# A batched GNN and GRU on one core: four batches in flight, and states turned by block transposes through device memory

## The chip, the core and the metric

The kernel runs on one core of a Trainium2 chip. The metric is device time in microseconds (us), from the start of the program to its end; lower is better. A core has five engines that run their own instruction streams and meet only at semaphores: TensorE (PE, matrix products, with its weight loads shown as PEld), VectorE (DVE), ScalarE (ACT), GpSimd (POOL) and SyncE (SP), which here only issues transfers (DMA).

## The reference

Sixteen batches of 512 nodes with 128 features. A first layer mixes each node with the mean of its neighbours, then a layer norm. Then five GRU layers in a row, each fed with the sum over a node's incoming edges; then a residual, the node mask and a second layer norm. All is float32.

```python
adj_norm = adj / (sum(adj, -1, keepdims) + 1e-8)
h = relu(concat([x, adj_norm @ x]) @ weight + bias)
x = layernorm(x + h)
A = (adj != 0)
h = x
for l in range(5):
    m = h @ weight[l]
    agg = einsum('bij,bid->bjd', A, m)
    gi = agg @ w_ih.T + b_ih;  gh = h @ w_hh.T + b_hh
    r = sigmoid(i_r + h_r);  z = sigmoid(i_z + h_z);  n = tanh(i_n + r * h_n)
    h = (1 - z) * n + z * h
out = layernorm(x + h * mask)
```

## The kernel before

Products are made from pairs of float32r parts: `x_hi` (a rounded copy, written by ACT) and `x_lo` (the rest, a subtraction on DVE or POOL). A product is then three matmuls, hi by hi, lo by hi and hi by lo. The weights of message and input gates are multiplied together at the start (`wc`), so a layer sums the states over the edges first.

The work is cut into **units**: one GRU layer of one batch. A unit on TensorE is 26 matmuls 512 columns wide: 8 for the edge sum into `ps_tok` (lines 1292 and 1299, stationary `tok_hi` and `tok_lo`, moving `edges`), 9 state products (`state_products`: `ps_hn`, `ps_r`, `ps_z` from `h_hi`, `h_lo`), and 9 gate products from `agg_hi`, `agg_lo` (`ps_r`, `ps_z`, `ps_in`). The other engines then do, for a unit:

- ACT: `agg_hi`, `r_gate`, `z_gate`, the tanh in `ps_in`, `h_hi` (not after layer 4), `tok_hi`;
- DVE: `agg_lo`, `r_hn`, `ps_in` plus `r_hn` (line 1020), (z - 1) n (line 1059), the new state `h` (line 962), `tok_lo`;
- POOL: `z_h` = z h (line 604) and `h_lo` (line 594, not after layer 4).

A state `h` lies with features on the partitions, while the next edge sum wants it with tokens (nodes) on the partitions. So TensorE turns it (line 1330: four 128x128 transposes against `ident` into `ps_tok`), ACT copies `tok_hi` out of the bank and DVE makes `tok_lo` from the bank. Only the last state of a batch goes another way: a DVE block transpose of 32x32 blocks (line 1131), one transfer to `passage` in device memory, and four transfers back to `last_rows` (lines 472 and 475), which together turn it whole.

A **window** has five slots, and each slot holds at most one unit. `UNITS` gives for each slot (how many batches back, which layer). A window also prepares the next batch: parts of its adjacency (`adjt_hi`, `adjt_lo`), its products, neighbour sums, row sums, layer norm (`x1`), the turned `x1` (`first_state` in slot 4) and its parts (`tok_lo` from `x1` on POOL at line 585, `h_lo[0]` at line 599). It also finishes an old batch (`pre2`, `stats2`, `cent2`, `y_out`). `FIRST_WINDOWS` and `LAST_WINDOWS` list the slots where batches are few. Windows 3 to 14 are one loop body. Every engine's order is the order of the code: each `window` function walks through the slots and tests conditions, and each engine waits at semaphores in that order. Two units of one batch have two units of others between them.

```python
UNITS = ((0, 0), (1, 2), (2, 4), (0, 1), (1, 3))
```

## Time and profile before

| | us |
|---|---|
| median of 3 runs (lowest, highest) | 625.54 (624.91, 625.80) |
| the profiled execution: its own time | 624.76 |
| its span (first to last instruction) | 623.0 |
| PE, DVE, ACT, POOL busy in the span | 604.4, 515.1, 411.3, 366.5 |

A row of a timeline gives start, duration, engine, line, operation and, in brackets, the idle time just before it with what ended it. A row of a group gives count, busy time and mean duration of one. TensorE's granted clock is full all through the middle of the span. Matmuls overlap their neighbours, so the step from one matmul to the next is the difference of their starts, not the duration shown.

### The profile page before, as it was taken

The page shows a single profiled execution, that of the slowest core. Times are in us where ns is not written, and L with a number is a line of the kernel's source. Part 1 is how long each engine was busy: PE and PEld are TensorE (multiplying, and loading weights), DVE is VectorE, ACT ScalarE, POOL GpSimd, SP SyncE. Part 2 cuts the span into 40 slices and gives each one's busy share as a digit, 9 for nine tenths or more (in the row PEclk, how much of TensorE's full clock was granted, in tenths as well). Part 3 has the DMA queues.
Part 4 walks back from the last instruction along what each step waited for, and adds up shares of the span by engine and source line. Part 5 has one row for each costly group of instructions (what it writes and reads, how often), then busy time and mean ns, then how long its engine had stood idle before and what let it go on. Part 6 is the DMA issues. An engine that isn't in the chain of part 4 may idle for free.

```text
span 623.0 us, 10141 instructions
## 1 busy us (share of the span) xinstructions
PE 604.4 (97%) x2877; PEld 492.6 (79%) x2877; DVE 515.1 (83%) x1177; ACT 411.3 (66%) x777; POOL 366.5 (59%) x299
## 2 busy tenths in 40 slices
PE   6999999999999999999999999999999999999993
PEld 5677888888888888888888888888888888887772
DVE  5987978897988879798897979889798887967677
ACT  4866776858667585766758576685866758564551
POOL 0644555757666575765658576576766657555343
PEclk9999999999999999999999999999999999999997
DMA  8531222231232323223231331333124131010101
GB/s 270 213 102 68 101 69 102 99 104 52 84 134 68 101 68 121 80 84 114 88 101 51 99 120 67 118 100 102 51 84 135 67 101 34 17 34 1 51 1 52
DMA packets 48080, 54.63 MB, mean 88 GB/s; under 512 B 2880, under 2 KB 27968, under 8 KB 48064
## 3 DMA queue, kind: packets, MB, share of 16 engines
q1 hardware_dynamic: 47792, 54.31, 26.3%
q8 instruction: 7, 0.11, 0.1%
q10 hardware_dynamic: 272, 0.13, 0.1%
q14 instruction: 9, 0.07, 0.0%
HBM read 46.57 MB, written 7.86 MB: 87 GB/s over the span
## 4 chain that ended last, share of the span: by engine, by line
PE 91%; DVE 4%; DMA 1%; ACT 1%; issue 1%; SPq 1%; POOL 0%; POOLq 0%; DVEq 0%
PE ps_tok L1292 12%; PE ps_tok L1299 12%; PE ps_r L1157 6%; PE ps_r L1158 6%; PE ps_r L1159 6%; PE ps_z L1159 6%; PE ps_z L1158 6%; PE ps_z L1157 6%; PE ps_tok L1152 5%; PE ps_b L1157 3%; PE ps_b L1158 3%; PE ps_b L1159 3%; PE ps_in L1157 3%; PE ps_hn L1159 3%; PE ps_in L1158 3%; PE ps_in L1159 3%
## 5 line engine op out<-in xcount | busy, mean ns | idle before, releaser
L594 POOL TENSOR_TENSOR h_lo<-h,h_hi 128x512 fp32r<-128x512 f32 x64 | 82.9, 1295 | 107.5 <-ACT h_hi L624 107.5
L604 POOL TENSOR_TENSOR z_h<-z_gate,h 128x512 f32<-128x512 f32 x80 | 110.0, 1374 | 43.1 <-ACT z_gate L801 43.1
L624 ACT ACTIVATE tok_hi<-ps_tok 128x512 fp32r<-128x512 f32 x63 | 37.7, 598 | 96.2 <-PE ps_tok L1152 96.2
L1292 PE MATMUL ps_tok<-edges,tok_hi 128*128 (+1 forms) x320 | 87.9, 397 | 0.7 <-ACT tok_hi L624 0.7
L1136 DVE SCALAR_TENSOR_TENSOR r_hn<-ps_hn,gru_bias,r_gate 128x512 f32<-128x512 f32 x80 | 59.9, 748 | 34.5 <-ACT r_gate L791 33.4
L1299 PE MATMUL ps_tok<-edges,tok_lo 128*128 (+1 forms) x320 | 87.7, 396 | 0.0
L724 ACT ACTIVATE ps_in<-ps_in,gru_bias 128x512 f32<-128x512 f32 x80 | 52.8, 660 | 52.8 <-DVE ps_in L1020 52.7
L544 POOL TENSOR_TENSOR adjt_lo<-adjt_in,adjt_hi 128x512 fp32r<-128x512 f32 x56 | 71.8, 1302 | 4.2 <-ACT adjt_hi L624 4.2
L1292 PEld LDWEIGHTS ps_tok<-edges,tok_hi 128*128 128x128 f32 x320 | 59.8, 188 | 15.4 <-ACT tok_hi L624 0.9
L1299 PEld LDWEIGHTS ps_tok<-edges,tok_lo 128*128 128x128 f32 x320 | 59.9, 188 | 14.8 <-DVE tok_lo L827 0.3
L827 DVE TENSOR_TENSOR tok_lo<-ps_tok,tok_hi 128x512 fp32r<-128x512 f32 x63 | 43.6, 692 | 27.9 <-ACT tok_hi L624 27.9
L1059 DVE SCALAR_TENSOR_TENSOR ps_in<-z_gate,ps_in 128x512 f32<-128x512 f32 x80 | 55.2, 690 | 11.9 <-ACT ps_in L724 10.6
L791 ACT ACTIVATE r_gate<-ps_r,rz_bias 128x512 f32<-128x512 f32 x80 | 54.9, 686 | 14.2 <-PE ps_r L1159 11.4
L1020 DVE TENSOR_TENSOR ps_in<-ps_in,r_hn 128x512 f32<-128x512 f32 x80 | 56.0, 700 | 8.0
L827 DVE TENSOR_TENSOR agg_lo<-ps_tok,agg_hi 128x512 fp32r<-128x512 f32 x80 | 55.0, 688 | 4.3 <-ACT agg_hi L624 4.3
L624 ACT ACTIVATE agg_hi<-ps_tok 128x512 fp32r<-128x512 f32 x80 | 47.9, 598 | 15.2 <-PE ps_tok L1299 14.1
L962 DVE TENSOR_TENSOR h<-z_h,ps_in 128x512 f32<-128x512 f32 x80 | 54.4, 680 | 1.2
L801 ACT ACTIVATE z_gate<-ps_z,rz_bias 128x512 f32<-128x512 f32 x80 | 55.0, 687 | 0.5
L624 ACT ACTIVATE h_hi<-h 128x512 fp32r<-128x512 f32 x77 | 48.1, 625 | 7.2 <-DVE h L962 7.1
L550 POOL TENSOR_TENSOR rstd<-var,minus_half 128x4 f32<-128x4 f32 x15 | 15.3, 1021 | 48.2 <-DVE var L925 48.2
L1152 PEld LDWEIGHTS ps_tok<-ident,h 128*128 128x128 f32 x252 | 30.7, 140 | 10.7 <-issue 2.3
L1152 PE MATMUL ps_tok<-ident,h 128*128 128x128 f32 x252 | 38.0, 273 | 0.7 <-DVE agg_lo L827 0.3
(146 smaller groups left out, 1574.2 us busy)
## 6 DMA issues: line engine op xcount, KB each, us to landing
adjt_in<-in_adj_t_dram SPq DMA_DIRECT2D x14, 1024.0 KB, 5.3
adj_in<-in_adj_dram SPq DMA_DIRECT2D x14, 1024.0 KB, 5.4
x_in<-in_x_dram SPq DMA_DIRECT2D x16, 256.0 KB, 2.8
xt_in<-in_x_t_dram SPq DMA_DIRECT2D x15, 256.0 KB, 2.6
out_dram<-y_out SPq DMA_DIRECT2D x15, 256.0 KB, 2.3
passage<-last_blocks SPq DMA_DIRECT2D x14, 256.0 KB, 2.0
last_rows<-passage SPq DMA_DIRECT2D x56, 64.0 KB, 2.0
adjt_in<-in_adj_t_dram SPq DMA_DIRECT2D x4, 256.0 KB, 4.6
```

Of the source, the lines that this page charges most:

```text
L544: nc.gpsimd.tensor_tensor(adjt_lo[:, j, :], adjt_in[:, j, :], raw(adjt_hi[:, j, :]), ALU.subtract).then_inc(s_adjt_lo, 1)
L594: nc.gpsimd.tensor_tensor(h_lo[new][:], h[new][:], raw(h_hi[new][:]), ALU.subtract).then_inc(s_h_lo, 1)
L604: nc.gpsimd.tensor_tensor(z_h[:], z_gate[:], h[own][:], ALU.mult).then_inc(s_zh, 1)
L624: return nc.scalar.activation(dst, src, ACT.Copy)
L827: return nc.vector.tensor_tensor(dst, src, raw(hi), ALU.subtract)
L1136: nc.vector.scalar_tensor_tensor(out=r_hn[:], in0=ps_hn[:], scalar=bhh_cols[:, 2:3], in1=r_gate[:], op0=ALU.add, op1=ALU.mult).then_inc(s_ ...
L1152: return nc.tensor.transpose(dst, src, ident[:])
L1157: nc.tensor.matmul(dst, lhs_hi, rhs_hi, start=start, stop=False)
L1158: nc.tensor.matmul(dst, lhs_hi, rhs_lo, start=False, stop=False)
L1159: return nc.tensor.matmul(dst, lhs_lo, rhs_hi, start=False, stop=stop)
L1292: nc.tensor.matmul(ps_tok[:], tok_hi[:, c * P:(c + 1) * P], edges_from(c, unit[0]), start=c == 0, stop=False)
L1299: last = nc.tensor.matmul(ps_tok[:], tok_lo[:, c * P:(c + 1) * P], edges_from(c, unit[0]), start=False, stop=c == C - 1)
```

## The change

Four batches are in flight: `UNITS` becomes layer 0 of the newest batch, layer 4 of the one three back, layer 3 of two back, layer 2 of one back and layer 1 of the newest, so that three units of others stand between two of a batch. The lists of first and last windows follow, windows 4 to 14 are the loop, and there is one window more. In windows 3 to 15 every unit in slots 1 to 4 (51 units) takes its tokens from a moved state: DVE transposes the blocks of each new state into one buffer `blocks`, SP sends them to `passage[k]` and fetches them to `rows[k]` (k is the layer they are for; 5 is the end), ACT makes `tok_hi` from `rows[k]` one slot ahead, and POOL makes `tok_lo`. TensorE's transposes of those units go, and so does DVE's `tok_lo`. The other 13 units of layers 1 to 4 are turned as before. The last state of batch 13 is now turned by TensorE, where it was moved before.

```diff
-UNITS = ((0, 0), (1, 2), (2, 4), (0, 1), (1, 3))
+UNITS = ((0, 0), (3, 4), (2, 3), (1, 2), (0, 1))
...
 FIRST_WINDOWS = (((0, 0), None, None, None, (0, 1)),
-                 ((0, 0), (1, 2), (0, 1), None, (1, 3)))
-LAST_WINDOWS = (((0, 0), (1, 2), (0, 1), (2, 4), (0, 2)),
-                ((2, 3), (1, 3), (2, 4), None, None),
-                (None, (2, 4), None, None, None))
+                 ((0, 0), (1, 2), (0, 1), None, (1, 3)),
+                 ((0, 0), (1, 2), (2, 4), (0, 1), None),
+                 ((0, 0), None, (2, 3), (1, 2), (0, 1)))
+LAST_WINDOWS = (((3, 4), (1, 2), None, None, None),
+                ((3, 3), (2, 3), (3, 4), None, None),
+                (None, (3, 4), None, None, None))
+FIRST_MOVED = ((2, 2), (2, 3), (2, 4), (3, 1), (3, 3), (3, 4))
...
+def is_moved(batches, n, slot):
+    return 3 <= n < batches and slot > 0
...
+            def pass_on(w, slot):
+                k = w.unit_before(slot)[1] + 1
+                sp.wait_ge(s_blocks, w.moved(slot))
+                sp.dma_start(passage[k][:], blocks[:].rearrange("p q c j -> p (q c j)")).then_inc(s_passed, 16)
+                sp.wait_ge(s_passed, w.value(lambda n: 16 * moved_states(B, n, slot)))
                 for q in range(Q):
...
+                    sp.dma_start(rows[k][q * SQ:(q + 1) * SQ, :, :, :].rearrange("i f c j -> i f (c j)"),
+                                 passage[k].rearrange("(f i) (q m) -> i f q m", f=Q, q=Q)[:, :, q, :]
+                                 ).then_inc(s_rows[k], 16)
...
+                if w.moves(0):
+                    pass_on(w, 0)
                 if w.loads():
...
                     load_xt(b)
+                if w.moves(1):
+                    pass_on(w, 1)
+                if w.loads():
                     sp.wait_ge(s_adjt_lo, w.prepared(C, C) if w.first > 0 else C)
                     load_adjt(b)
+                if w.moves(2):
+                    pass_on(w, 2)
...
+                if w.moves(3):
+                    pass_on(w, 3)
                 if w.loads():
...
                     load_x(b)
...
                     load_adj(b)
+                if w.moves(4):
+                    pass_on(w, 4)
...
+                    if w.next_moved(slot):
+
+                        pool.wait_ge(s_tok_hi, w.turned(slot + 2))
+                        nc.gpsimd.tensor_tensor(tokens(tok_lo), rows_by_tokens(w.unit(slot + 1)[1]),
+                                                tokens(raw(tok_hi[:])), ALU.subtract).then_inc(s_tok_lo, 1)
...
+            def row_sum_of(c, of, earlier):
+
+                if earlier is not None:
+                    act.wait_ge(s_row_sum, earlier)
...
+                    if w.next_moved(slot):
+
+                        k = w.unit(slot + 1)[1]
+                        act.wait_ge(s_rows[k], w.rows(4 * 16, k))
+                        evacuate(tokens(tok_hi), rows_by_tokens(k)).then_inc(s_tok_hi, 1)
...
+                    if w.moves(slot):
+
+                        dve.wait_ge(s_h, w.units(slot))
+                        if w.first > 2 or slot > 0:
+                            dve.wait_ge(s_passed, w.value(lambda n: 16 * (moved_states(B, n, slot) - 1)))
+                        nc.vector.transpose(blocks[:].rearrange("p q c j -> p c q j"),
+                                            h[w.home_made(slot)][:].rearrange("p (c q j) -> p c q j", c=C, q=Q)
+                                            ).then_inc(s_blocks, 1)
...
-                    if unit:
+                    if unit and w.next_turned(slot):
                         pe.wait_ge(s_agg_lo, w.units(slot + 1))
...
                         wi_hi, wi_lo = wc_hi[:, layer, :], wc_lo[:, layer, :]
+                        pe.wait_ge(s_agg_lo, w.units(slot + 1))
```

Beside these, the four scratch copies of the row sums become one (so each row sum waits for the one before it), `stats1` in slot 3 comes whole behind `agg_lo`, `pre2` moves from slot 1 to slot 0, and the finishing of a batch comes one window later.

On TensorE, in slot 2 of the loop, from the last state product to the gate products, before:

```order
L1159 MATMUL ps_z<-h_hi4,whh_lo 128x512
...
L1152 MATMUL ps_tok<-ident,h1 128x128 [waits s_h,s_agg_lo]
L1152 MATMUL ps_tok<-ident,h1 128x128 x3
L1157 MATMUL ps_r<-agg_hi,wc_hi 128x512
L1158 MATMUL ps_r<-agg_lo,wc_hi 128x512
```

and now:

```order
L1240 MATMUL ps_z<-h_hi3,whh_lo 128x512
...
L1238 MATMUL ps_r<-agg_hi,wc_hi 128x512 [waits s_agg_lo]
L1239 MATMUL ps_r<-agg_lo,wc_hi 128x512
```

The four transposes are gone, and the gate products wait for `agg_lo` themselves. The same holds in slots 0, 1 and 3.

On TensorE, at the end of window 2, from the gates of slot 3 on (`h3` is a state that slot 4 turns into tokens), before:

```order
L1152 MATMUL ps_tok<-ident,h3 128x128 [waits s_h,s_agg_lo]
L1152 MATMUL ps_tok<-ident,h3 128x128 x3
L1157 MATMUL ps_r<-agg_hi,wc_hi 128x512
...
L1157 MATMUL ps_in<-agg_hi,wc_hi 128x512 [waits s_h]
...
L1292 MATMUL ps_tok<-edges,tok_hi 128x512 [waits s_tok_lo]
L1292 MATMUL ps_tok<-edges,tok_hi 128x512 x3
L1299 MATMUL ps_tok<-edges,tok_lo 128x512 x4
L1157 MATMUL ps_hn<-h_hi3,whh_hi 128x512 [waits s_rhn,s_h_lo]
```

and now, over the end of window 2 into slot 0 of window 3 (`x1` is the new batch's first state):

```order
L1238 MATMUL ps_in<-agg_hi,wc_hi 128x512 [waits s_h]
...
L1233 MATMUL ps_b1<-ident,x1 128x128 [waits s_x1]
L1233 MATMUL ps_b1<-ident,x1 128x128 x3
L1370 MATMUL ps_tok<-edges,tok_hi 128x512 [waits s_x1_hi,s_edges]
L1370 MATMUL ps_tok<-edges,tok_hi 128x512 x3
L1377 MATMUL ps_tok<-edges,tok_lo 128x512 [waits s_x1_lo]
L1377 MATMUL ps_tok<-edges,tok_lo 128x512 x3
L1238 MATMUL ps_hn<-h_hi0,whh_hi 128x512 [waits s_rhn,s_h0_lo]
```

The whole unit of slot 4 is gone from between the gates of slot 3 and the new batch's first unit. Slot 1 of window 3 likewise has only its neighbour sums left.

On GpSimd, in slots 2 and 3 of the loop, before:

```order
L559 TENSOR_TENSOR rstd2<-var2,minus_half 128x4 [waits s_var2]
L563 TENSOR_TENSOR cent2<-pre2,mv2 128x512
...
L567 TENSOR_TENSOR y_out<-cent2,rstd2 128x512 [waits s_cent2]
...
L594 TENSOR_TENSOR h_lo3<-h3,h_hi3 128x512 [waits s_h_hi]
...
L604 TENSOR_TENSOR z_h<-z_gate,h4 128x512 [waits s_z]
...
L550 TENSOR_TENSOR rstd1<-var1,minus_half 128x4 [waits s_var1]
...
L604 TENSOR_TENSOR z_h<-z_gate,h1 128x512 [waits s_z]
```

and now:

```order
L649 TENSOR_TENSOR tok_lo<-rows2,tok_hi 128x512 [waits s_tok_hi]
...
L618 TENSOR_TENSOR rstd2<-var2,minus_half 128x4 [waits s_var2]
L622 TENSOR_TENSOR cent2<-pre2,mv2 128x512
...
L626 TENSOR_TENSOR y_out<-cent2,rstd2 128x512 [waits s_cent2]
...
L668 TENSOR_TENSOR z_h<-z_gate,h3 128x512 [waits s_z]
L649 TENSOR_TENSOR tok_lo<-rows1,tok_hi 128x512 [waits s_tok_hi]
...
L609 TENSOR_TENSOR rstd1<-var1,minus_half 128x4 [waits s_var1]
...
L658 TENSOR_TENSOR h_lo4<-h4,h_hi4 128x512 [waits s_h_hi]
...
L668 TENSOR_TENSOR z_h<-z_gate,h2 128x512 [waits s_z]
```

A `tok_lo` stands at the head of both slots, and the `h_lo` of slot 2 is now in slot 3, behind `rstd1` and ahead of `z_h` (on ACT its `h_hi` now stands in slot 3 ahead of `r_gate`).

## Rows read from the trace of the kernel before

**Rows 1.** The page, its head and its section 1.

```profile
span 623.0 us, 10141 instructions
...
PE 604.4 (97%) x2877; PEld 492.6 (79%) x2877; DVE 515.1 (83%) x1177; ACT 411.3 (66%) x777; POOL 366.5 (59%) x299
```

**Rows 2.** Busy time of each engine in two stretches: window 2, and one loop window.

```profile
core 0: us, PE busy (x) PEld busy (x) DVE busy (x) ACT busy (x) POOL busy (x), PEclk, DMA share, GB/s
71.00:108.30 37.30, 37.30 (x180) 30.61 (x180) 30.65 (x61) 27.31 (x53) 20.69 (x17) 1.00 0.23 79
300.90:337.87 36.97, 36.97 (x180) 30.44 (x179) 31.57 (x73) 25.55 (x49) 23.84 (x19) 1.00 0.29 92
```

**Rows 3.** Timeline of PE: the turn in slot 2; slots 3 and 4 begin.

```profile
314.50 0.60 PE L1152 MATMUL ps_tok<-ident,h 128*128 128x128 f32 x4
314.85 0.48 PE L1157 MATMUL ps_r<-agg_hi,wc_hi 128*128 128x512 f32 x1
315.16 0.40 PE L1158 MATMUL ps_r<-agg_lo,wc_hi 128*128 128x512 f32 x1
315.40 0.40 PE L1159 MATMUL ps_r<-agg_hi,wc_lo 128*128 128x512 f32 x1
...
317.02 1.10 PE L1292 MATMUL ps_tok<-edges,tok_hi 128*128 x4
...
323.49 1.10 PE L1292 MATMUL ps_tok<-edges,tok_hi 128*128 x4
```

**Rows 4.** Groups of one shape: the turn, `tok_lo`, the block transpose, a GpSimd subtraction.

```profile
L1152 PE MATMUL ps_tok<-ident,h 128*128 128x128 f32 x252 | 38.0, 273 | 0.7 <-DVE agg_lo L827 0.3
L827 DVE TENSOR_TENSOR tok_lo<-ps_tok,tok_hi 128x512 fp32r<-128x512 f32 x63 | 43.6, 692 | 27.9 <-ACT tok_hi L624 27.9
L1131 DVE STREAM_TRANSPOSE last_blocks<-h 128x512 f32<-128x512 f32 x14 | 9.9, 706 | 0.0
L594 POOL TENSOR_TENSOR h_lo<-h,h_hi 128x512 fp32r<-128x512 f32 x64 | 82.9, 1295 | 107.5 <-ACT h_hi L624 107.5
```

**Rows 5.** The page, section 6: transfers, KB each, us to landing.

```profile
adj_in<-in_adj_dram SPq DMA_DIRECT2D x14, 1024.0 KB, 5.4
...
passage<-last_blocks SPq DMA_DIRECT2D x14, 256.0 KB, 2.0
last_rows<-passage SPq DMA_DIRECT2D x56, 64.0 KB, 2.0
```

**Rows 6.** Timeline of SP: issues of one moved state.

```profile
328.36 0.35 SPq L472 DMA_DIRECT2D passage<-last_blocks  x1
330.41 1.76 SPq L475 DMA_DIRECT2D last_rows<-passage  x4
```

**Rows 7.** Timeline: slot 4 and the start of slot 0.

```profile
324.48 1.43 DVE L931 TENSOR_SCALAR x<-pre,mv,rstd 128x128 f32<-128x128 f32 x4
...
326.43 0.69 DVE L827 TENSOR_TENSOR agg_lo<-ps_tok,agg_hi 128x512 fp32r<-128x512 f32 x1
...
326.75 1.29 POOL L585 TENSOR_TENSOR tok_lo<-x,tok_hi 128x512 fp32r<-128x512 f32 x1 [1.70 <-ACT tok_hi L624]
...
327.03 0.68 DVE L962 TENSOR_TENSOR h<-z_h,ps_in 128x512 f32<-128x512 f32 x1
...
327.74 0.63 ACT L624 ACTIVATE h_hi<-h 128x512 fp32r<-128x512 f32 x1 [0.55 <-DVE h L962]
327.78 0.48 PE L1157 MATMUL ps_r<-agg_hi,wc_hi 128*128 128x512 f32 x1
...
330.04 1.30 POOL L599 TENSOR_TENSOR h_lo<-h,h_hi 128x512 fp32r<-128x512 f32 x1 [0.29 <-ACT h_hi L624]
...
331.82 0.39 PE L1157 MATMUL ps_hn<-h_hi,whh_hi 128*128 128x512 f32 x1
```

**Rows 8.** Timeline of POOL: `adjt_lo` of a window's second half, slot 1.

```profile
302.43 2.56 POOL L544 TENSOR_TENSOR adjt_lo<-adjt_in,adjt_hi 128x512 fp32r<-128x512 f32 x2
```

**Rows 9.** Line 948 (`edges`): shortest, median and longest in ns; one pair in slot 1.

```profile
L948 DVE TENSOR_SCALAR edges<-adj_in x56: 412/421/1443, 55.0 to 536.8; 128x512 f32 x48, 128x512 fp32r<-128x512 f32 x8
...
308.25 1.67 DVE L948 TENSOR_SCALAR edges<-adj_in 128x512 f32 x2
```

More of the change, by code:

```diff
@@ L306, in program @@
         Q = P // SQ
-        last_blocks = sb("last_blocks", [P, Q, C, SQ])
-        passage = nc.dram_tensor("passage", [P, N], F32, kind="Internal").ap()
-        last_rows = sb("last_rows", [P, Q, C, SQ])
+        KINDS = range(1, LAYERS + 1)
+        blocks = sb("blocks", [P, Q, C, SQ])
+        passage = {k: nc.dram_tensor(f"passage{k}", [P, N], F32, kind="Internal").ap() for k in KINDS}
+        rows = {k: sb(f"rows{k}", [P, Q, C, SQ]) for k in KINDS}
         ps_tok = bank("ps_tok")
@@ L406, in all_windows @@
         def all_windows(window, eng):
-            for n in range(3):
+            for n in range(4):
                 window(Window(B, n))
-            with eng.Fori(0, B - 4) as trip:
-                window(Window(B, 3, trip))
-            for n in range(B - 1, B + 3):
+            with eng.Fori(0, B - 5) as trip:
+                window(Window(B, 4, trip))
+            for n in range(B - 1, B + 4):
                 window(Window(B, n))
@@ L1052, in window @@
                         low_part(agg_lo[:], ps_tok[:], agg_hi[:]).then_inc(s_agg_lo, 1)
+                    if slot == 1 and w.ends_by_rows() and not w.prepares():
+                        stats2_of_batch()
                     if slot == 2 and w.idles():
@@ L1062, in window @@
                         new_state(slot)
-                    if w.unit(slot) and not before_candidate(w, slot):
-                        dve.wait_ge(s_agg_hi, w.units(slot + 1))
+                    if w.summed(slot) and not before_candidate(w, slot):
+                        v, s = w.summed(slot)
+                        dve.wait_ge(s_agg_hi, v.units(s + 1))
                         low_part(agg_lo[:], ps_tok[:], agg_hi[:]).then_inc(s_agg_lo, 1)
```

174 lines of the change are left out of this document (90 added, 84 removed).

## The prediction

> **What bounds the kernel now.** I read the page's head first: TensorE is busy for 604.4 of 623.0 us [rows 1], the next engine, DVE, for 515.1. Then the busy time by stretch: in a loop window TensorE is busy for all of its 36.97 us, and in window 2 for all of 37.30 [rows 2]. There is no wait to remove; in the middle of the span only fewer or shorter matmuls help. DVE has 5.4 us to spare in a loop window and POOL 13.1 [rows 2]. I call the start of slot s of a window Ts. In the loop window shown T1 is 300.90 [rows 2], T3 317.02, T4 323.49 [rows 3]. The time of the profiled execution is 624.76, 1.76 above its span and 0.8 below the median of the runs, 625.54.
>
> **The turns that go.** The turn of slot 2 starts at 314.50 and the second matmul behind it at 315.16, which is 0.66; one step between matmuls is 0.24 (315.16 to 315.40), so four transposes cost 0.42 [rows 3]. The group gives 38.0 us for 252, so 0.60 for four with the overlap counted [rows 4]; the steps of the timeline are the real price, and I take 0.44, since the neighbouring matmul steps average 0.23 (slot 3 is 26 steps and a turn, and lasts 6.47 [rows 3]: 6.47 less 26 times 0.232 is 0.44). 51 units lose their turn, and one last state gains one: 50 x 0.44 = **22.0 us less** for TensorE. A loop window would go from 36.97 to 35.2. Bounds are 21 (0.42) and 23 (0.46).
>
> **What takes their place.** Per loop window:
> - DVE swaps four `tok_lo` of 692 ns for four block transposes of 706 ns [rows 4]. That is 0.06 more, 31.6 in 35.2 us. A transpose stands directly behind `h` where `tok_lo` stood a little later, so the order hardly changes. Nothing added.
> - POOL gets four `tok_lo`. The nearest row is its other subtraction of that shape, 1295 ns [rows 4]; so 5.2 more, 29.0 in 35.2 us. It reads `rows[k]` in runs of 32 elements, which no POOL row shows; I take the same price, with 0.2 more each as the upper bound.
> - ACT makes `tok_hi` from another place, at about the same price, and no longer waits for a turn.
> - SP: one moved state issues from 328.36 to 332.17 (330.41 and 1.76) and the last rows land 2.0 later [rows 5, 6], so 5.8 us from the issue. `blocks` is ready some 5 us into a slot and ACT reads `rows[k]` nearly 3 us into the second slot after it: in slots of 6 to 8.8 us that is 10 us or more. The worst case is the state handed over in slot 4: slot 3's transfers are issued to about T4 + 3.5, the 1 MB `adj_in` load follows and takes 5.4 [rows 5], and the write to `passage` is queued behind it. Written at T4 + 10.5, fetched by T4 + 14.5, wanted at T4 + 17. The next transpose waits for that write (one buffer) and comes at T4 + 10.9. Both hold, the second by 0.4. Nothing added, and 1 us in each loop window as the upper bound.
>
> **Two missing units.** All 80 units are still done, but window 2 has none in slot 4 and window 3 none in slot 1, and those units covered waits. Window 2, slot 4: the next thing TensorE can do is the new batch's unit. In a loop window its parts are ready as follows, from T4 = 323.49 [rows 7]: `x1` at 325.91 (+2.4), `tok_lo` of it at 328.04 (+4.6), `h_lo[0]` at 331.34 (+7.9). Without a unit ACT skips `agg_hi`, `r_gate` and `z_gate`, so I take +7.2 for the last. Until then TensorE has one turn and one edge sum, 0.44 + 8 x 0.23 = 2.3. It waits 4.9. Window 3, slot 1: `adjt_lo` of the second half is done at 304.99, which is T1 + 4.1 [rows 8]; three matmuls follow, so the slot lasts 4.8, and TensorE has 12 x 0.23 = 2.8 of work. It waits 2.0. Together **7 us more**. Bounds: 4, if the engines behind run early in these emptier windows, and 9. In window 2 before, there was no wait at all [rows 2]. The last seven units are the same as before and in the same order, so I expect the tail unchanged.
>
> **The steady windows.** Slots are 0.44 shorter, and two places come close. In slot 3 an `h_hi` (625 ns before, as in the row at 327.74 [rows 7]) now stands on ACT ahead of `r_gate`, since the unit before it is layer 3 and no longer the last. It pushes `r_gate`, then `r_hn`, then through slot 4's DVE order everything: `x1`, `agg_lo`, `h`, by about 0.6. In slot 4 before, `agg_lo` ended at 327.12 and the gates began at 327.78, so 0.6 in hand; `h_lo[0]` ended at 331.34 and was wanted at 331.82, so 0.5 in hand [rows 7]. POOL is the second: it now reaches slot 4 with `h_lo` and `z_h` of slot 3 still to do, just when DVE makes `x1`. What DVE then pays is shown by the `edges` group: 412 ns at the shortest and 421 in the median, but 1443 at the longest, and a pair started at 308.25 took 1.67 [rows 9] beside a POOL instruction. I charge 0.5 us for both in each of the 12 windows with this slot 4 (3 to 14): **6 us more**. Bounds: nothing, and 1.3 each (a whole POOL instruction [rows 4]), 15.6.
>
> A rule bears on this. The Trainium skill (SBUF — State Buffer, Who interferes with whom) says that GpSimd and a DVE instruction in its two-port mode, `tensor_scalar` among them, take one shared port pair in turn, and that one fully blocks while the other runs. By that rule, with a POOL instruction in the way every time, this term is at its upper bound and the result 626.1 (625.5 - 22.0 + 7.0 + 15.6), on the side of rival 2; where POOL happens to be idle it is nothing. The spread from 412 to 1443 agrees with it, the median says that it is rare so far.
>
> **The sum.** -22.0 + 7.0 + 6.0 = -9.0 us: 624.76 - 9.0 = 615.8 for a profiled execution, and with the 0.8 between it and the median **616.5**. The forecast's own range is 609 to 621.
>
> **The rivals.**
> 1. The empty slots and the tight places cost little. Then nearly all of the 22.0 is kept: 603.5, with the lower bound of the ramp (4) 607.5. For it: the waits of slots 4 are only some tenths by rows 7, and POOL has much to spare. Against it: x1's chain in slot 4 is shown to take 7.9 us and cannot start earlier than its own statistics. Chance 0.17.
> 2. GpSimd becomes what the others wait for, and it comes out slower. The place is POOL's order at the end of slot 3 and in slot 0: `tok_lo` ahead of `z_h`, and behind `z_h` DVE's `h`, which is ahead of the block transpose, `x1` and `r_hn`, and TensorE's `ps_in` gate. Price: up to 1.3 a place. After the 7 us of the ramp 15 are left, over 12 windows 1.25 each; from a stall of 1.25 us in each window on, the change loses, and at 1.6 it stands at 629.7. For it: POOL goes from 64% to 82% of a window, and DVE stands at 90%. Against it: `z_h` has over an us in hand in most slots. A late `rows[k]` would look alike in time, but ends ACT's wait by a DMA. Chance 0.14, both places together.
> 3. The same stalls, but milder: 0.9 to 1.25 in each window, so 621 to 625.5. Chance 0.14, half of it within 0.2% of before.
> 4. The forecast, 0.55.
>
> A measurement of this kernel can tell about 0.2% (1.25 us) from no change. Faster is 0.55 + 0.17 + 0.07 = 0.79, same 0.07, slower 0.14. The range that should hold 8 of 10 goes from 606, which leaves out the lower part of rival 1, to 625, which leaves out rival 2.
>
> **What would show it.** In the changed kernel's profile:
> - 204 fewer transposes into `ps_tok`, and slots of TensorE without waits at 6.03 (slot 3), 6.46 (slot 4) and 8.8 us (slot 1). If the slots do not shorten, the 0.44 is wrong.
> - TensorE idle for about 5 us at the end of window 2, released by `h_lo[0]` or `tok_lo` on POOL, and 2 us in slot 1 of window 3. If it is busy there, rival 1.
> - A loop window of about 35.7 us, with TensorE waiting some tenths in slots 4 and 0, released by DVE's `agg_lo` and POOL's `h_lo[0]`. Over 36.4: rival 2 or 3; the largest waits then name `z_h` (POOL), `edges` or `x1` with a long mean (the ports), or `tok_hi` with a DMA before it (SP).
> - `blocks` transposes that start late with SP as releaser would show that the single buffer is the bound.
>
> The forecast is wrong if DVE, not TensorE, has no idle time in the loop window, or if the block transpose or the POOL subtraction takes clearly more than 0.71 and 1.3 us.

## The result, and the profile after

The changed kernel takes **662.1 us** (661.1 to 662.3, 4 runs) against 625.2 (624.9 to 625.8) of the kernel before: 1.0585 times, interval 1.0567 to 1.0604. The forecast was 616.5. It is 5.9% slower where 1.4% faster was expected.

The page of the changed kernel, head and section 1 (answers to [rows 1]):

```profile
span 660.2 us, 10087 instructions
...
PE 606.3 (92%) x2677; PEld 468.7 (71%) x2677; DVE 571.0 (86%) x1176; ACT 411.6 (62%) x777; POOL 432.7 (66%) x350
```

200 matmul records are gone, as they should be (50 turns of four less), and TensorE's busy time has still not fallen: a matmul is recorded as about 0.39 us long and the next starts 0.23 us later, so short waits are hidden under the recorded busy time. DVE gained 55.9 us (515.1 before) though its list of work was meant to stay the same, and POOL 66.2 (366.5 before), as much as the 51 new subtractions (66.5). Next, busy time by stretch: windows 2 and 3, one loop window, and then the five slots of another loop window (answers to [rows 2]):

```profile
core 0: us, PE busy (x) PEld busy (x) DVE busy (x) ACT busy (x) POOL busy (x), PEclk, DMA share, GB/s
71.15:105.56 34.41, 31.15 (x149) 25.28 (x149) 29.28 (x59) 23.80 (x46) 18.03 (x15) 0.99 0.22 68
105.56:140.26 34.70, 31.80 (x138) 24.71 (x137) 25.29 (x50) 22.39 (x44) 22.26 (x18) 0.96 0.47 151
305.93:345.39 39.46, 36.98 (x163) 28.38 (x162) 36.08 (x73) 25.39 (x49) 29.06 (x24) 1.00 0.43 142
337.60:345.39 7.79, 7.71 (x39) 6.24 (x38) 7.38 (x10) 7.01 (x14) 7.20 (x6) 1.00 0.47 162
345.39:354.79 9.40, 9.03 (x40) 7.05 (x39) 8.63 (x24) 6.78 (x17) 7.04 (x7) 1.00 0.29 84
354.79:361.96 7.17, 6.76 (x32) 5.22 (x30) 6.54 (x13) 3.98 (x7) 4.71 (x5) 1.00 0.58 183
361.96:368.97 7.01, 6.53 (x28) 4.64 (x27) 6.53 (x15) 2.71 (x6) 4.46 (x4) 1.00 0.38 112
368.97:377.05 8.08, 6.95 (x31) 5.22 (x30) 6.99 (x15) 4.92 (x10) 5.72 (x5) 1.00 0.54 177
```

The loop window (the first of the three columns behind the stretch is its length) is 39.46 us against 36.97, with DVE busy for 36.08 of it against 31.57. Where did 4.5 us of DVE come from? By line, shortest, median and longest in ns, and by group (answers to [rows 4] and [rows 9]):

```profile
L1049 DVE SCALAR_TENSOR_TENSOR pre<-rows,mask_cols,x_kept x52: 307/1380/1389, 145.4 to 612.9; 128x128 f32<-128x128 f32 x52
L1004 DVE TENSOR_SCALAR x<-pre,mv,rstd x64: 332/340/1341, 19.4 to 571.8; 128x128 f32<-128x128 f32 x64
...
L1049 DVE SCALAR_TENSOR_TENSOR pre<-rows,mask_cols,x_kept 128x128 f32<-128x128 f32 x52 | 51.8, 1055 | 0.0
L1004 DVE TENSOR_SCALAR x<-pre,mv,rstd 128x128 f32<-128x128 f32 x64 | 38.1, 656 | 0.2
L1162 DVE STREAM_TRANSPOSE blocks<-h 128x512 f32<-128x512 f32 x64 | 45.6, 712 | 7.4 <-DMA passage<-blocks 0.3
L649 POOL TENSOR_TENSOR tok_lo<-rows,tok_hi 128x512 fp32r<-128x512 f32 x51 | 66.5, 1304 | 48.2 <-ACT tok_hi L688 48.2
```

The new operations cost what was forecast: the transpose 712 ns, the GpSimd subtraction 1304. Nearly all of the 4.5 us is in two **unchanged** operations that got longer. The four instructions of `pre2` (`pre<-rows,...`) last 1380 ns in the median, though 307 is possible; those of `x1` (`x<-pre,...`) reach 1341, though 332 is possible. In a loop window `pre2` grew by 3.2 us and `x1` by 1.3; `edges` (also `tensor_scalar`) grew by 0.45, from a mean of 708 ns to 820; what else changed on DVE is smaller. The timeline of slot 0 and slot 4 shows what stands beside the first two:

```profile
341.58 2.65 POOL L603 TENSOR_TENSOR adjt_lo<-adjt_in,adjt_hi 128x512 fp32r<-128x512 f32 x2 [0.31 <-ACT adjt_hi L688]
342.14 0.71 DVE L1162 STREAM_TRANSPOSE blocks<-h 128x512 f32<-128x512 f32 x1
342.77 4.21 DVE L1049 SCALAR_TENSOR_TENSOR pre<-rows,mask_cols,x_kept 128x128 f32<-128x128 f32 x4
344.20 1.33 POOL L649 TENSOR_TENSOR tok_lo<-rows,tok_hi 128x512 fp32r<-128x512 f32 x1
345.50 1.34 POOL L658 TENSOR_TENSOR h_lo<-h,h_hi 128x512 fp32r<-128x512 f32 x1
346.80 1.33 POOL L668 TENSOR_TENSOR z_h<-z_gate,h 128x512 f32<-128x512 f32 x1
...
370.46 1.29 POOL L658 TENSOR_TENSOR h_lo<-h,h_hi 128x512 fp32r<-128x512 f32 x1
370.85 2.75 DVE L1004 TENSOR_SCALAR x<-pre,mv,rstd 128x128 f32<-128x128 f32 x4
371.71 1.29 POOL L668 TENSOR_TENSOR z_h<-z_gate,h 128x512 f32<-128x512 f32 x1
```

GpSimd runs without a gap, and the four `pre2` take 4.21 us in place of 1.4. Taken singly, the first lasts 0.31 us, and each of the other three 1.38, ending 0.15 us after an instruction of GpSimd (which end at 344.2, 345.5 and 346.8). Of the four `x1`, two last 0.98 and 1.33 us and end with a GpSimd instruction; the two behind them, with GpSimd idle, last 0.33. None of this shows as a wait of DVE: it stands in its busy time, and in the eleven windows from 140.26 to 575.60 no wait of DVE is ended by GpSimd. What shows is TensorE waiting for DVE, where the kernel before has no wait at all (total in the eleven windows, times, longest, in us):

```profile
PE ps_r L1238 <- DVE agg_lo L900: 15.8, 33, 0.5
PE ps_b L1233 <- DVE x L1004: 6.6, 11, 0.6
PE ps_b L1238 <- DVE own L911: 5.3, 11, 1.6
```

The Trainium skill (SBUF — State Buffer, Who interferes with whom) names both forms: the two-port mode of `tensor_scalar`, and any DVE instruction with two inputs in SBUF beside a GpSimd instruction that reads SBUF; "Issue order, not op shape, decides who blocks". `pre2` is of the second kind, `x1` of the first, and both rows agree.

The waits in the ramp, where windows 2 and 3 have a slot without a unit (in brackets the wait and who ended it):

```profile
104.75 1.06 PE L1233 MATMUL ps_b<-ident,x 128*128 128x128 f32 x4 [3.26 <-DVE x L1004]
109.41 0.50 PE L1238 MATMUL ps_hn<-h_hi,whh_hi 128*128 128x512 f32 x1 [0.52 <-POOL h_lo L663]
118.06 0.47 PE L1238 MATMUL ps_b<-adjt_hi,y_hi 128*128 128x512 f32 x1 [1.39 <-POOL adjt_lo L603]
119.22 0.50 PE L1238 MATMUL ps_b<-adjt_hi,y_hi 128*128 128x512 f32 x1 [0.22 <-POOL adjt_lo L603]
```

The first of these waits costs more than its 3.26 us. Right behind it, from 104.90 to 108.30, TensorE's granted clock is 0.50, the lower of its two levels (1.2 GHz), and the four matmuls from 105.56 to 107.41 take 1.85 us where those of a loop window take 0.94:

```profile
104.90:108.30 3.40, 3.40 (x11) 2.70 (x11) 1.80 (x3) 3.19 (x6) 2.76 (x3) 0.50 0.72 202
```

Half speed for 3.4 us is at most 1.7 us of TensorE's work. The kernel before, which does not wait there, has the full clock over the same time.

The transfers (answers to [rows 5]; KB each, us to landing) kept their pace: those that fetch the rows land in 2.0 us as before, and only the large load takes longer (6.7 for 5.4), beside four and a half times as many passages:

```profile
passage<-blocks SPq DMA_DIRECT2D x64, 256.0 KB, 2.0
...
adj_in<-in_adj_dram SPq DMA_DIRECT2D x14, 1024.0 KB, 6.7
```

And where the 37.2 us of the span are: the 11 windows 4 to 14 begin and end with these rows, first of the kernel before, then of the changed one:

```profile
145.12 1.10 PE L1292 MATMUL ps_tok<-edges,tok_hi 128*128 x4
551.75 1.10 PE L1292 MATMUL ps_tok<-edges,tok_hi 128*128 128x512 f32 x4
```

```profile
140.26 1.10 PE L1370 MATMUL ps_tok<-edges,tok_hi 128*128 x4
575.60 1.09 PE L1370 MATMUL ps_tok<-edges,tok_hi 128*128 128x512 f32 x4
```

That is 406.6 us before and 435.3 after, 28.7 more; what lies around them (span less these) went from 216.4 to 224.9, 8.5 more. The loop window is 39.58 us in the mean of the eleven, against 36.97.

### The profile page after: what moved, and what is told of

Read it like the earlier page. It is cut to its first block, busy times and chain, and to the rows that moved or that the text cites. A ratio compares the mean times of both kernels' runs of the same rounds, so it can differ in the third digit from the quotient of the medians.

```text
span 660.2 us, 10087 instructions
## 1 busy us (share of the span) xinstructions
PE 606.3 (92%) x2677; PEld 468.7 (71%) x2677; DVE 571.0 (86%) x1176; ACT 411.6 (62%) x777; POOL 432.7 (66%) x350
## 4 chain that ended last, share of the span: by engine, by line
DVE 42%; PE 20%; issue 17%; ACT 9%; POOL 7%; DMA 2%; DVEq 1%; SPq 1%; POOLq 0%; ACTq 0%
DVE pre L1049 6%; DVE ps_in L1093 5%; DVE r_hn L1217 5%; DVE x L1004 5%; DVE h L1035 5%; POOL z_h L668 3%; ACT ps_in L792 3%; PE ps_tok L1370 3%; DVE edges L1021 3%; PE ps_tok L1377 3%; ACT sum_of L700 2%; DVE ps_b L975 2%; POOL h_lo L658 2%; DVE stats L991 2%; DVE ps_in L1133 2%
## 5 line engine op out<-in xcount | busy, mean ns | idle before, releaser
L649 POOL TENSOR_TENSOR tok_lo<-rows,tok_hi 128x512 fp32r<-128x512 f32 x51 | 66.5, 1304 | 48.2 <-ACT tok_hi L688 48.2
L1093 DVE TENSOR_TENSOR ps_in<-ps_in,r_hn 128x512 f32<-128x512 f32 x80 | 55.9, 699 | 8.0
L1238 PE MATMUL ps_r<-agg_hi,wc_hi 128*128 128x512 f32 x80 | 36.4, 455 | 17.0 <-DVE agg_lo L900 16.9
L1162 DVE STREAM_TRANSPOSE blocks<-h 128x512 f32<-128x512 f32 x64 | 45.6, 712 | 7.4 <-DMA passage<-blocks 0.3
L1049 DVE SCALAR_TENSOR_TENSOR pre<-rows,mask_cols,x_kept 128x128 f32<-128x128 f32 x52 | 51.8, 1055 | 0.0
L1021 DVE TENSOR_SCALAR edges<-adj_in 128x512 f32 (+1 forms) x56 | 43.2, 795 | 0.0
```

What stands on the lines that cost most here:

```text
L1049: last = nc.vector.scalar_tensor_tensor(out=pre[:, c, :].rearrange("p (f j) -> p f j", f=Q), in0=rows[LAYERS][:, :, c, :] if w.ends_by_row ...
L1093: nc.vector.tensor_tensor(ps_in[:], ps_in[:], r_hn[:], ALU.add).then_inc(s_npre, 1)
```

## The experiments

Each kernel was run beside the kernel before, at 624.6 to 625.1 us. All slot lengths below are steps between the first aggregation matmuls of the slots, as means over the 11 windows. In the expectations, theories P and C both say that DVE's instructions last longer beside GpSimd's, and that this is the loss; theory R lays the loss to something else, mostly to the block transposes and DVE's work as such. O and "Rival O" are said in their places.

**Where `pre2` stands.** The working had not priced that the change moves `pre2` from slot 1 to slot 0. Two kernels: the changed one with `pre2` back in slot 1, and the kernel before with it in slot 0.

```
-                    if slot == 0 and w.ends_by_rows():
+                    if slot == (1 if w.prepares() else 0) and w.ends_by_rows():
                         pre2_of_batch()
```

> The changed kernel with one move: in the windows that prepare a batch, pre2 (four VectorE instructions with two SBUF inputs) goes from slot 0 back to slot 1, where GpSimd has a gap of 2 us. Theory P (VectorE waits for GpSimd at SBUF: the four take 4.2 us instead of 1.1 because GpSimd runs without a gap there, and VectorE is the bound of the window): the four fall to about 1.4 us, a loop window from 39.46 to 36.7, in all 12 x 2.8 less: about 630 us. Theory R (VectorE is the bound because of the block transposes and the waits around them, wherever pre2 stands): at most 0.5 us a window less, 655 or more.

Measured: **670.0 us** (ratio 1.0725, 1.0708 to 1.0743), slower still. Theory P missed by 40 us; the time lies in the open range of theory R (655 or more), but the window grew by 0.67 us, which R did not say either. Slot 1 had no free place to offer: in it `pre2` meets the next GpSimd instructions (this is the timeline of that kernel):

```profile
353.89 3.26 DVE L1049 SCALAR_TENSOR_TENSOR pre<-rows,mask_cols,x_kept 128x128 f32<-128x128 f32 x4
354.03 1.34 POOL L649 TENSOR_TENSOR tok_lo<-rows,tok_hi 128x512 fp32r<-128x512 f32 x1
355.71 1.29 POOL L658 TENSOR_TENSOR h_lo<-h,h_hi 128x512 fp32r<-128x512 f32 x1 [0.33 <-ACT h_hi L688]
```

The four take 3.26 us in place of 4.21, and still the kernel is slower. Slot 1 came down to 8.74, all of it TensorE's own work, but slot 2 rose from 7.20 to 8.60: there the delay meets a shorter slot. So the length of the contended instructions alone does not give the loss; where the delay lands counts too.

The kernel before, the other way round:

```
-                    if slot == 1 and w.finishes() and not w.idles():
+                    if slot == (0 if w.moves() and w.prepares() else 1) and w.finishes() and not w.idles():
                         pre2_of_batch()
```

> The kernel before with one move: in its loop windows pre2 goes from slot 1 to slot 0. Theory P: GpSimd runs adjt_lo and h_lo there, so each of the four takes up to 1.3 us (mean 700 to 1200 ns instead of 344), VectorE goes from 31.6 to 34 us a window, which the 5.4 us to spare mostly cover: 625 to 634 us. Theory R: pre2 stays at 344 ns and the time at 625.

Measured: **632.2 us** (1.0114, 1.0097 to 1.0131): the move alone costs the kernel before 7 us, within theory P's 625 to 634. Slot 0 went from 7.91 to 8.36, and in the eleven windows a `pre2` instruction lasts 889 ns in the mean against 343 (P: 700 to 1200). The line in that kernel, over all of its 56 instructions:

```profile
L976 DVE SCALAR_TENSOR_TENSOR pre<-last_rows,mask_cols,x_kept x56: 339/473/1382, 112.6 to 602.7; 128x128 f32<-128x128 f32 x56
```

**The order of units alone.** Four batches in flight, but all states but the last turned by TensorE and their low parts on DVE.

```
 def is_moved(batches, n, slot):
-    return 3 <= n < batches and slot > 0
+    return False
```

> The changed kernel with four batches in flight and its slots, but TensorE turns all states as before, only the last state of a batch is moved, and GpSimd makes no token low parts. Theory P: pre2 still stands in slot 0, beside only three GpSimd instructions instead of six, so half of the loss: window 37.5, and 7 us for the first windows: 637 to 642. Theory R (transposes): window as before, 36.97, and the 7 us: 632. If four in flight cost nothing: 625.

Measured: **649.6 us** (1.0398, 1.038 to 1.0415). A miss of both theories (637 to 642, and 632): 24 us more than the kernel before, with none of the new block transposes and none of the new GpSimd work. Its slots are 8.73, 9.30, 6.97, 6.56, 6.84 against 7.91, 9.21, 6.92, 6.47, 6.46 before. What of it is the order and what contention is taken up below.

**The low parts on DVE.** GpSimd's four `tok_lo<-rows` moved to DVE.

```
-                        nc.gpsimd.tensor_tensor(tokens(tok_lo), rows_by_tokens(w.unit(slot + 1)[1]),
+                        nc.vector.tensor_tensor(tokens(tok_lo), rows_by_tokens(w.unit(slot + 1)[1]),
                                                 tokens(raw(tok_hi[:])), ALU.subtract).then_inc(s_tok_lo, 1)
```

> The changed kernel with the token low parts of the moved units on VectorE instead of GpSimd. Theory P: GpSimd loses 5.2 us a window and pre2 falls to 1.1 to 2.5 us, x1 to 1.5, but VectorE gets four subtractions of 0.7 us, so VectorE's sum hardly changes, 35.5 to 36.5 us: 645 to 662 us, with pre2's mean clearly under 1055 ns. Theory R: VectorE gets 2.8 us more a window and nothing back: 690 us, and pre2's mean stays at 1055 ns.

Measured: **705.5 us** (1.1287, 1.1264 to 1.131), slower by 43 us than the changed kernel, and above both theories (645 to 662, and 690). The change was right to give them to GpSimd. The line in that kernel, over 110 us of its middle:

```profile
L1194 DVE TENSOR_TENSOR tok_lo<-rows,tok_hi x11: 691/1768/1819, 289.2 to 393.6; 128x512 fp32r<-128x512 f32 x11
```

Read from PSUM, as in the kernel before, the same subtraction took 692 ns [rows 4]. Read from two SBUF tiles it takes 691 at the shortest and 1768 in the median. `pre2` did get shorter (854 ns in the mean of the eleven windows, 1138 in the changed kernel), as theory P had said, but the four new subtractions take 6.0 us a window where 2.8 were added up. So a state that comes back through memory costs DVE more than its transpose: it also loses the PSUM source that had kept its low part clear of GpSimd.

**Less GpSimd, less transpose.** The first kernel leaves out all but a sixteenth (32 of 512 columns; the expectation says a 32nd) of each moved low part, the second turns one block of 32 columns in place of sixteen.

```
-                        nc.gpsimd.tensor_tensor(tokens(tok_lo), rows_by_tokens(w.unit(slot + 1)[1]),
+                        nc.gpsimd.tensor_tensor(tokens(tok_lo)[:, 0:1, 0:1, :], rows_by_tokens(w.unit(slot + 1)[1])[:, 0:1, 0:1, :],
```

> The changed kernel, but GpSimd makes only a 32nd of each moved unit's token low part (128x16 of... one block of 32 tokens in place of all 512), so the state's low parts are wrong and the time is that of a kernel without GpSimd's four 1.30 us instructions a window. Theory C (VectorE instructions with two SBUF inputs or the two-port form last longer beside GpSimd instructions; measured so far: pre2 1151 ns each against 343, x1 747 against 420): with 5 us less of GpSimd in a window they fall to near the row of the kernel before, the window goes from 39.46 to 37 to 38, the time to 632 to 645. Theory R (the four block transposes, and the instructions that wait behind them, are the price): nothing of VectorE's own work goes, the time stays at 655 or more.

Measured: **650.9 us** (1.0416, 1.0392 to 1.0439), 11 less, between the two theories. DVE instructions by group in the middle of that kernel:

```profile
L1049 DVE SCALAR_TENSOR_TENSOR pre<-rows,mask_cols,x_kept 128x128 f32<-128x128 f32 x28 | 23.2, 887 | 0.0
L1004 DVE TENSOR_SCALAR x<-pre,mv,rstd 128x128 f32<-128x128 f32 x28 | 19.3, 747 | 0.0
```

`x1` did not profit at all: its neighbours are `h_lo` and `z_h`, and those are GpSimd's in any case. So the new GpSimd work is a part of the cause only; the other part is when DVE comes by: in a window of this kernel two of the four `pre2` still take 1.38 us, where in the changed kernel three do.

```
-                        nc.vector.transpose(blocks[:].rearrange("p q c j -> p c q j"),
-                                            h[w.home_made(slot)][:].rearrange("p (c q j) -> p c q j", c=C, q=Q)
-                                            ).then_inc(s_blocks, 1)
+                        nc.vector.transpose(blocks[:, 0, 0, :], h[w.home_made(slot)][:, 0:SQ]).then_inc(s_blocks, 1)
```

> The changed kernel, but each block transpose turns one 32-column block of the state instead of all sixteen, so the moved states are wrong and the time is that of a kernel with VectorE relieved of 5 times about 0.65 us a window; GpSimd's work stays whole. Theory R: this is the price, window 36 to 37, time 620 to 635. Theory C: the contended instructions still take 7.5 us a window where the kernel before spends 3.1, of VectorE's 36.1 busy us only 3.2 go, and the time comes to 640 to 652.

Measured: **641.2 us** (1.026, 1.0243 to 1.0277), 20.9 less, where theory C had said 10 to 22 and theory R 27 or more. DVE's time counts, but slots 0 to 2 stay as in the changed kernel (7.80, 9.48, 7.19); only 3 and 4 shorten (6.02, 7.52). In slot 3, 6.02 is TensorE's own work, and `h_hi` still stands ahead of `r_gate` there.

**An input in PSUM.** The direct test: take away what makes the two instructions wait. In the first kernel the residual instruction writes its sum back into the matmul bank that it reads (except in the first windows), and the statistics and `x1` read it there. In the second, ScalarE copies the last state's rows to a free bank, from which `pre2` reads.

```
+            def pre1_at(w):
+                return pre1[:] if w.ramps() else ps_b[0][:].rearrange("p (c d) -> p c d", c=C)
...
-                nc.vector.scalar_tensor_tensor(out=pre1[:], in0=ps_b[0][:].rearrange("p (c d) -> p c d", c=C),
+                nc.vector.scalar_tensor_tensor(out=pre1_at(w), in0=ps_b[0][:].rearrange("p (c d) -> p c d", c=C),
...
-                    nc.vector.tensor_scalar(x1[:, c, :], pre1[:, c, :], mv1[:, c, 0:1],
+                    nc.vector.tensor_scalar(x1[:, c, :], pre1_at(w)[:, c, :], mv1[:, c, 0:1],
```

> The changed kernel with the residual sum of a prepared batch left in its PSUM bank, so that x1 is read from PSUM and not from SBUF; the values are the same. Theory C: x1 falls from 747 ns to about 350 and no longer depends on GpSimd; slot 4 of a window (8.09 us from one aggregation to the next) comes down to 6.8 to 7.3, the window by 0.8 to 1.3, the time to 645 to 652. Theory R: x1 is not what the others wait for; 658 to 663.

Measured: **649.4 us** (1.0431, 1.0366 to 1.0497). Slot 4 went from 8.10 to 6.69. The residual and the statistics, which the edit touches too, changed little (680 to 689 ns, 274 to 282), and the other slots hardly moved, but for one: a slot 1 of the profiled execution lasted 13.20 us, with a TensorE wait of 2.76 us and then a granted clock of 0.50 for 3.4 us. The four runs lie between 647.7 and 656.8 us, so the 12.7 us less are good to a few us only.

```
+                        act.wait_ge(s_rows[LAYERS], w.finished(4 * 16, 4 * 16))
+                        evacuate(ps_b[2][:], rows[LAYERS][:].rearrange("p f c j -> p (f c j)")).then_inc(s_copied, 1)
...
-                            in0=rows[LAYERS][:, :, c, :] if w.ends_by_rows() else
+                            in0=ps_b[2][:].rearrange("p (f c j) -> p f c j", f=Q, c=C)[:, :, c, :] if w.ends_by_rows() else
```

> The changed kernel with one more ScalarE instruction a window (about 0.6 us) that copies the last state's rows into a free PSUM bank, so that pre2 has one input in SBUF and one in PSUM; the values are the same. Theory C: pre2 falls from 1151 ns to about 350, VectorE's busy time in a window by 3 us, slot 1 from 9.39 to 8.8 and slot 0 or 2 by some tenths, the time to 640 to 652. Theory R: pre2 is covered by TensorE's own work in slots 0 and 1; 656 to 663.

Measured: **638.7 us** (1.0227, 1.021 to 1.0244), 23.4 less from 13 ScalarE instructions more, and a little better than theory C's 640 to 652. Slots 1, 2 and 3 went to 8.74, 6.48 and 6.52. Not every collision went: beside GpSimd's `h_lo` the first `edges` of slot 1 fell from 1.47 us to 0.39, and a small `var` ahead of it rose from 0.17 to 1.2.

Both together:

> The changed kernel with both moves of an input to PSUM: x1 read from the bank of the residual sum (alone: 12.7 us less than the changed kernel), and the last state's rows copied to a free bank for pre2 (alone: 23.4 us less). Theory C (VectorE's instructions wait for GpSimd's where they need the port that both use, and each such wait stands on its own place in the window): the slots' lengths add up as 7.79, 8.75, 6.48, 6.53, 6.69, a window of 36.24 us against 36.97 of the kernel before, and the time is 662.1 - 12.7 - 23.4 = 626, from 621 to 628. Rival O (the two waits cover each other, or a common limit such as VectorE's sum of work takes over): 632 to 639.

Measured: **622.6 us** (0.9969, 0.996 to 0.9979): faster than the kernel before, by 0.3%. The slots are 7.79, 8.74, 6.47, 6.53, 6.69, a window of 36.24, as the expectation had added them. The two lines, and one window of this kernel:

```profile
L1058 DVE SCALAR_TENSOR_TENSOR pre<-ps_b,mask_cols,x_kept x64: 307/340/351, 144.5 to 612.3; 128x128 f32<-128x128 f32 x64
L1013 DVE TENSOR_SCALAR x<-ps_b,mv,rstd x52: 398/403/407, 102.4 to 532.8; 128x128 f32<-128x128 f32 x52
```

```profile
319.26:355.48 36.22, 36.03 (x163) 28.66 (x162) 32.34 (x72) 25.71 (x51) 28.20 (x24) 1.00 0.48 153
```

No `pre2` lasts over 351 ns and no `x1` over 407, with GpSimd as busy as ever (28.2 us in a window of 36.2). Nor did they merely move to a quiet time: in the eleven windows all 44 `x1` and all 44 `pre2` instructions have GpSimd at work beside them from start to end. From PSUM an uncontended `x1` is 63 ns longer than from SBUF (403 against 340), a good trade for not waiting a microsecond. That settles the main cause: the two together gave back 39.5 us, more than the 36.9 that the change had lost.

**Statistics behind the state, in slot 3.** Added to `both_psum`:

```
-                    if w.prepares() and slot == 3 and not w.ramps():
-                        stats1_of(range(C), pre1_at(w))
-                        dve.wait_ge(s_stats1, w.prepared(C, C))
                     if slot == 4 and w.first == 1:
                         new_state(slot)
                         norm1(w)
                     if w.unit_before(slot) and not (slot in (0, 2, 4) and w.first == 1):
                         new_state(slot)
+                    if w.prepares() and slot == 3 and not w.ramps():
+                        stats1_of(range(C), pre1_at(w))
+                        dve.wait_ge(s_stats1, w.prepared(C, C))
```

> The same as both_psum, with the four statistics of slot 3 behind the new state instead of ahead of it. In the changed kernel h waits for 0.86 us of statistics in slot 3, its TF32-like high part stands ahead of r_gate on ScalarE, and r_gate came 1.05 us after its sum was done. If that order is what slot 3 has over 6.03 us (it has 6.53 without the pre2 contention), slot 3 comes down to 6.0 to 6.2 and the time by 3 to 6 us below both_psum, so 616 to 623; if the chain behind it (moments, rstd, x1) then ends slot 4 later by as much, the time stays as in both_psum.

Measured: **621.4 us** (0.9939, 0.9922 to 0.9956), some 2 us under `both_psum` by the ratios, not 3 to 6. Slot 3 went from 6.53 to 6.42, so the statistics ahead of the state, and with them a late `h_hi`, are not what holds it. DVE's sum of work there is the better reading (6.07 busy of 6.54 us in slot 3 of `both_psum`), and the kernels with the cut transposes bear it out: with 0.5 us less of DVE work in slot 3 and the orders untouched it is 6.02 and, below, 6.03, TensorE's own length.

**What the order costs.** The same two moves to PSUM in the kernel with the order alone.

> sched_only (four batches in flight, all but the last state turned by TensorE, none of the new low parts on GpSimd) with both moves to PSUM. Theory C: the 24.4 us that the order of units cost there is contention too (pre2 964 ns, x1 582), so the window falls from 38.39 to 36.9 to 37.2 and the time from 649.6 to 630 to 635, the rest over 624.8 being the slots without work in windows 2 and 3. Theory O: units three slots apart cost in themselves; the time stays at 640 or more.

Measured: **644.1 us** (1.0317, 1.0301 to 1.0334), in the range of theory O: slot 4 went to 6.46, as before, but slot 0 stood at 8.77. Its timeline shows a third contended instruction, and who had put it there:

```profile
332.36 1.31 POOL L669 TENSOR_TENSOR z_h<-z_gate,h 128x512 f32<-128x512 f32 x1
332.68 1.54 DVE L906 TENSOR_TENSOR xt_lo<-xt_in,xt_hi 128x512 fp32r<-128x512 f32 x1 [0.58 <-ACT xt_hi L689]
...
335.54 0.66 PE L1242 MATMUL ps_tok<-ident,h 128*128 128x128 f32 x4 [0.63 <-DVE agg_lo L906]
```

The same place in the kernel before:

```profile
331.09 0.80 DVE L827 TENSOR_TENSOR xt_lo<-xt_in,xt_hi 128x512 fp32r<-128x512 f32 x1
331.29 1.76 POOL L604 TENSOR_TENSOR z_h<-z_gate,h 128x512 f32<-128x512 f32 x1
```

There `xt_lo` starts 0.2 us ahead of `z_h`, takes 0.80, and `z_h` pays (1.76 in place of 1.3). In `sched_psum` my ScalarE copy, at the head of slot 0, made `xt_hi` 0.6 us later; `z_h` was first, and `xt_lo` took 1.54. So the copy was moved behind `agg_hi` and `tok_hi` of slot 0 (from the head of the slot's branch to the place ahead of `if w.next_turned(slot)`), in that kernel and in `both_psum`.

> sched_psum with the same move of the copy. There TensorE turns a state in slot 0 and waited 0.63 us for agg_lo, which stood behind xt_lo of 1.53 us. Theory C: slot 0 falls from 8.77 to 7.9 to 8.1, the window to that of the kernel before, 36.97 to 37.2, and the time from 644.1 to 632 to 636: then the order of units itself costs nothing but the slots without work in windows 2 and 3. Theory O (three units between two of a batch cost in slot 0 by themselves): 640 or more.

Measured: **634.8 us** (1.0155, 1.014 to 1.0169), theory C, and slot 0 is 7.90. One window of it:

```profile
297.17:334.27 37.10, 37.10 (x180) 30.33 (x178) 31.46 (x73) 26.51 (x50) 23.79 (x19) 1.00 0.29 92
```

TensorE is busy in all of it: with these contentions gone, three units between two of a batch cost next to nothing in a loop window (37.10 against 36.97). Of the 10.4 us by which its span is longer (633.4 against 623.0), 1.5 are in the eleven windows and 8.9 around them (225.3 against 216.4). The slots without a unit are there, and 3.4 us at the granted clock 0.50 (105.0 to 108.4) behind a TensorE wait of 2.8 us; how the 8.9 divide is not shown.

> both_psum with ScalarE's copy of the rows moved behind agg_hi and tok_hi of slot 0 instead of at the slot's head. In both_psum the copy pushed xt_hi back by 0.6 us, VectorE's xt_lo then started after GpSimd's z_h and lasted 1.52 us, where in the kernel before it started 0.2 us ahead of z_h and lasted 0.80 while z_h lasted 1.76: whoever starts first holds the other. Theory C: xt_lo is back at 0.8 us. Whether the time moves is a second question: if xt_lo is what slot 0 waits for (7.77 us, 7.49 needed), 618 to 620; if it is the chain to h_lo of the first state, which was the same in the changed kernel (slot 0 7.79 with xt_lo at 0.79), 621.5 to 623.5.

Measured: **621.1 us** (0.9938, 0.9922 to 0.9955). `xt_lo` is back at 797 ns and slot 0 still 7.80 us: the second of the two answers written down, though the time is 0.4 us below its range, since slot 3 gained 0.2. The rows agree that slot 0 waits for the chain to `h_lo` of the first state: in the window from 320.17 `h_lo` ends at 322.14 and the first state product starts at 322.28, a quarter of a us later than the matmul steps alone would have it. Slot 3 went to 6.33 and slot 4 stayed at 6.69. With `both_psum_late`, which it equals within the intervals, it is the fastest kernel here that leaves nothing out: 0.6% under the kernel before, 41 us under the change as it was made.

> copy_later with the block transposes cut to one block of 32 columns (212 ns in place of 712), so the moved states are wrong. With pre2 and x1 uncontended VectorE has some 32.3 busy us in a window of 36.2. If its own work no longer sets the pace, the transposes cost little: 1 to 4 us less than copy_later (in the changed kernel the same cut gave 20.9 us). If VectorE still sets it, 8 us less or more.

Measured: **613.3 us** (0.9817, 0.9802 to 0.9831): 7.8 less than `copy_later`, where the same cut had given 20.9 in the changed kernel. That is more than the 1 to 4 of a DVE with room, just short of the 8 of one that sets the pace: DVE's own work is the third part of the loss. In a window:

```profile
323.47:358.96 35.49, 35.46 (x164) 28.79 (x163) 29.37 (x73) 26.17 (x50) 28.72 (x24) 1.00 0.49 159
```

TensorE is busy throughout, in slots of 7.75, 8.74, 6.47, 6.03 and 6.48: but for 0.28 in slot 0 this is the window of 35.2 us that the forecast had started from.

## Why the prediction was wrong, step by step

- **The turns that go: held.** Slots without waits were forecast at 6.03 (slot 3), 6.46 (slot 4) and 8.8 (slot 1); the last kernel has 6.03, 6.48 and 8.74. Against the kernel before, slots 1, 2 and 3 are 0.47, 0.45 and 0.44 shorter, where 0.44 was taken; only slot 0 gained no more than 0.16, held by `h_lo`.
- **What takes their place: this step failed**, in the words "Nothing added" for DVE. The prices of the new instructions were right (712 for 706, 1304 for 1295), SP and the rows were in time (the transposes waited 0.3 us in all for `passage`), ACT was as told. But the sum of 31.6 us in a window took every unchanged DVE instruction at its old duration. `pre2` was not in the working at all, neither its move to slot 0 nor its price, which was to triple (343 to 1138 ns in the mean). Measured in the window: 36.08.
- **The steady windows: right kind, wrong size.** Contention was charged at 0.5 us a window together with `h_hi`, up to 1.3, as one GpSimd instruction in the way of `x1`. In the changed kernel `x1` met two (2.75 us for 1.43) and `pre2` met three (4.21 for 1.4). Eleven windows grew by 2.6 each over the kernel before, 4.4 over the 35.2 hoped for: 48 us, where 6, at most 15.6 in twelve, was charged. Of the 4.4, `pre2` is 1.9 (39.58 to 37.63 with its input in PSUM), `x1` 1.4 (slot 4), the time of the block transposes on a full DVE 0.6 (36.04 to 35.48), `h_lo` in slot 0 0.3; these add up to 4.2. The median of `edges`, 421 ns in [rows 9], was read as a sign that collisions are rare. The kernel before says otherwise if one window is asked for (from 300.9 to 337.9):

```profile
L948 DVE TENSOR_SCALAR edges<-adj_in x4: 415/536/1336, 308.3 to 315.0; 128x512 f32 x4
```

In each of its eleven windows the four `edges` last some 1340, 415, 655 and 420 ns, and the first `x1` lasts 655 for 340. So collisions came in every window of the kernel before too. The median over the whole kernel hid them, and they cost nothing there, since TensorE had no wait. The rule of the Trainium skill that the prediction weighed pointed the right way; its result, 626.1, fell short because it was worked out for one collision a window, at `x1`.
- **`h_hi` ahead of `r_gate` in slot 3: no cost.** In `small_transpose` and `copy_later_small_tr` it stands there as before, and slot 3 lasts 6.02 and 6.03, no more than TensorE's own work.
- **Two missing units: held in size.** TensorE waited 3.26 + 0.52 + 1.39 + 0.22 = 5.4 us there, for 6.9 forecast (bounds 4 and 9), and for `x1` first, not for `h_lo[0]`. Not in the working was the clock: at most 1.7 us more behind the first wait. Around the eleven windows the span grew by 8.5, where 7 less some 3 (six or seven turns) was implied. With both inputs in PSUM it is 4.4 (`both_psum`) and 7.0 (`copy_later`), the first with one such stretch of 3.4 us at the granted clock 0.50, as in the changed kernel, the second with two; how much of the rest is contention is not shown.
- **The rivals.** Rival 2 had the sign and the engine, and its threshold of 1.25 us a window, but not the way: `z_h` was not late for `h`; in the eleven windows DVE has no wait that ends with GpSimd. GpSimd was waited for inside DVE's own instructions. At 0.14, with an end at 629.7, it was both too unlikely and too cheap. The closing sentence, "The forecast is wrong if DVE, not TensorE, has no idle time in the loop window", half came. DVE is what TensorE waits for, busy for 36.08 of 39.46 us, and in slots 0 and 3 for 7.38 of 7.79 and 6.53 of 7.01. But it has idle time: 3.4 us a window, more than the 2.5 in which TensorE is seen idle.

## What to carry to other kernels

When a change gives work to GpSimd, go through VectorE's list, not GpSimd's: every instruction there with two SBUF inputs, or an fp32 `tensor_scalar` from SBUF to SBUF, can grow by a whole GpSimd instruction each time the two meet, and the four small ones of a group can pay three times (4.21 us for 1.4). Price each as if it met one, unless the trace shows GpSimd idle at the new time, and take its shortest and longest duration and ask how often each comes in one window, not its median over the whole kernel. If one such input can come from PSUM, even by a copy on an engine with time to spare, that can be cheaper than reordering: moving `pre2` made things worse both times, and a 0.6 us copy took its whole wait away. Look also at where the copy goes: at the head of slot 0 it made a third instruction collide.
